# q, k and the shared expert's first products, from plain F32 to three F32R products each

## The chip, the cores and the metric

The kernel runs on one core of a Trainium2 chip, as one launch. The metric is the device time of that launch in microseconds. TensorE has two clock levels, 1.2 and 2.4 GHz; the profile gives the granted one as a share of the higher.

## The reference, cut to what matters

The model has two layers over x of shape (8, 512, 256). Only the first layer is touched:

```python
h = _layernorm(x, axis=-1) * (1 + ca) + sa
# attention of layer 0
normed = (h - mu) * rsqrt(var + LN_EPS) * ln_g + ln_b
hh = silu(normed @ W_hidden + b_hidden)      # 256 -> 1024: v and gate
qk = silu(normed @ W_qk + b_qk)              # 256 -> 512
q = qk * os_gamma[0] + os_beta[0]
k = qk * os_gamma[1] + os_beta[1]
sim = einsum('bid,biD->bdD', q, k) / seq_len
attn = softmax(sim, axis=-1)
out = v * sum(attn, axis=-1)[:, None, :] * gate
x = x + ga * (out @ W_out + b_out + h)
# experts of layer 0
h = _layernorm(x, axis=-1) * (1 + cb) + sb
shared_out = silu(h @ sw1) * (h @ sw3) @ sw2           # 256 -> 512 -> 256
# router: sigmoid(h @ router_w.T), top 2 of 8 experts, gates from their scores
# routed: gelu(h @ ew1[e]) @ ew2[e], 256 -> 256 -> 256, weighted by the gates
x = x + gb * (shared_out + routed_out)
```

The second layer is a state-space scan (512 channels, 16 states) and a gated MLP with ternary weights.

## The kernel before

Work goes by batch, 512 tokens each, eight batches in each layer. Each engine has one queue of instructions, laid when the program is built. A stage of a batch is a generator that yields a place (a due time) ahead of each piece of work; `in_order` merges all stages of an engine by these places, so the constants in `PLAN`, `PLAN_A` (first layer) and `PLAN_LAST` (its last batch's experts) fix the order and nothing else. Data is handed on by semaphores; waits stand in the code ahead of each instruction. A piece whose place is smaller than that of the one before it in the same stage follows it at once.

One batch of the first layer, on TensorE: `att_tensor` turns the normed tokens (`xhatA`, line 229), makes q/k products (four tiles of 128 tokens, line 234), the hidden products (eight tiles, lines 765 to 767), `sim` (four tiles) and the output products (`wo`). `ffn_tensor` turns `xhatF`, makes the router's products, the shared expert's first two matrices (`shared(m)`, four tiles each of `s1` and `s3`), the ranks of the routed tokens, and the shared expert's second matrix (line 1107). `experts_tensor` goes through 15 tiles of 128 routed tokens in eight pairs: step i transposes the tokens of pair i (line 1135), makes the first products of pair i-1 and the second of pair i-2. The expert steps of a batch are interleaved with the attention of the next one; those of the last batch run beside the start of the second layer.

The hidden products are already made in three F32R products. F32R (float32r) is a rounded form of float32 that TensorE takes as operand. The weights are parted once into `w_hidH` (rounded to F32R) and `w_hidL` (the rest), the input per batch into `nTH` and `nTL`, and a product is

```python
pe.matmul(bank[:, :], w_hidH[:, k, of], nTH[:, k, :], start=(k == 0), stop=False)
pe.matmul(bank[:, :], w_hidL[:, k, of], nTH[:, k, :], start=False, stop=False)
i = pe.matmul(bank[:, :], w_hidH[:, k, of], nTL[:, k, :], start=False, stop=(k == KD - 1))
```

The activation engine (ACT) makes `nT` (float32) and `nTH`; GpSimd subtracts them for `nTL` (line 681) and adds `b_out` rows to `h_tok`, multiplies and adds the k rows (`k_tok`, lines 693 and 697). DVE does the norms, the bias of q/k (line 632), the q rows (lines 636 and 640), the maxima of `sim` (line 645), the gated rows (line 656), the routing (lines 887 to 968), the product of the shared tiles (line 977) and the combination of the routed results (lines 1001 to 1006).

Routing: `slots` (line 968) releases eight indirect scatters on GpSimd (line 860) that write the normed tokens by expert into DRAM. SP loads them back as `xs` (line 815) for the expert steps; results go to DRAM as `eo_rows` (line 821), and eight indirect gathers (line 868) bring them to their tokens, for the combination. Expert weights are fetched by SP for each tile into one of `WE` = 6 buffers `w_exp`, the first matrix (line 839) when the first products of tile w - WE are done, the second (line 845) when its second products are.

PSUM banks go round in rings of four, one for attention (`att_bank`, in the order of `ATT`), one for the experts (`ffn.take`): each take waits until the reader of four tiles ago is done. `rowsA` holds a batch's shift, scale and gate rows, two buffers. `w_hid` lies in expert buffers before it is parted.

## Time and profile before

| | |
|---|---|
| Time, median of 3 runs | 2521.0 us (2517.49 to 2522.68) |
| Profiled execution, its own time | 2522.81 us |
| Its span in the trace | 2521.1 us |
| TensorE (PE) busy | 2271.8 us, 90% |
| DVE, ACT, GpSimd (POOL) busy | 1706.7, 1395.1, 1329.0 us |
| Mean granted clock of TensorE | 0.949 |

The first layer takes about the first third of the span: the last batch's tokens for attention are turned at 726.9 us, and the second layer's scans begin at 873.3 us. Times in rows are from the span's start. PE is a matmul, PEld its weight load, which lies beside it. The end of a matmul is modelled, so the pace is read from start to start.

### The profile page before, as it was taken

To read this page: it belongs to the slowest core of one execution; us is meant where nothing else is said; L and a number is where in the kernel's file an instruction comes from. 1 tells how busy PE (TensorE), PEld (TensorE's weight loads), DVE (VectorE), ACT (ScalarE), POOL (GpSimd) and SP (SyncE) were. 2 spreads that over 40 slices of the span, in tenths; PEclk is the share of its full clock that TensorE was granted. 3 is DMA by queue.
4 is the path that set the end of the run, shared out by engine and by line. 5 is a ranking of instruction groups with operands and counts; after the bars stand their busy time and mean duration, and the time that the engine had idled before them with its cause. 6 is when DMAs were issued, how large, how long until landed. Compare 5 with 4: busy or idle time off the path is not lost. (4 is left out here: it accounts for less than half of the span.)

```text
span 2521.1 us, 27219 instructions
## 1 busy us (share of the span) xinstructions
PE 2271.8 (90%) x8584; PEld 1477.0 (59%) x8584; DVE 1706.7 (68%) x2735; ACT 1395.1 (55%) x1872; POOL 1329.0 (53%) x1152
## 2 busy tenths in 40 slices
PE   7899999999999867689979989989989998988978
PEld 3576776766766532245645645655655654655666
DVE  6465655545654488996896796797787788687630
ACT  3244343443443555467677677767767667766622
POOL 4225234243251254666666665765755756767733
PEclk9899999999999987889989999999999999999989
DMA  7165465554544644545645645744744645546622
GB/s 255 64 191 174 142 200 164 179 169 135 171 143 149 217 140 132 134 125 162 170 114 162 167 127 152 186 124 137 194 116 137 185 120 155 173 125 175 167 77 92
DMA packets 253775, 384.53 MB, mean 153 GB/s; under 512 B 19168, under 2 KB 160112, under 8 KB 253632
## 3 DMA queue, kind: packets, MB, share of 16 engines
q1 hardware_dynamic: 223408, 281.07, 39.0%
q0 software_dynamic: 30224, 101.73, 13.0%
q8 instruction: 69, 1.13, 0.2%
q14 instruction: 74, 0.61, 0.1%
HBM read 345.67 MB, written 47.55 MB: 156 GB/s over the span
## 5 line engine op out<-in xcount | busy, mean ns | idle before, releaser
L1508 POOL TENSOR_TENSOR d_in<-u,bc 128x512 f32<-128x512 f32 x512 | 656.4, 1292 | 356.0 <-DMA bc<-bc_rows 294.6
L1518 DVE TENSOR_TENSOR_SCAN bank<-bank,d_in 128x512 f32<-128x512 f32 x512 | 625.9, 1222 | 114.4 <-ACT bank L1574 85.2
L1596 PE MATMUL bank<-w_st,ident 128*128 128x512 f32 x1024 | 541.3, 643 | 88.0 <-DVE w_st L1526 87.6
L1574 ACT ACTIVATE bank<-dt,a_neg 128x512 f32<-128x512 f32 x512 | 347.4, 688 | 398.3 <-DVE w_st L1526 396.7
L1526 DVE TENSOR_TENSOR w_st<-bank,bc 128x512 f32<-128x512 f32 x512 | 345.1, 674 | 136.4 <-PE bank L1596 136.0
L240 PE MATMUL bank<-f1H,w_ring 128*128 128x512 f32 x768 | 355.2, 463 | 37.0 <-POOL f1L L1674 16.1
L1596 PEld LDWEIGHTS bank<-w_st,ident 128*128 128x128 f32 x1024 | 196.6, 201 | 306.8 <-DVE w_st L1526 173.6
L241 PE MATMUL bank<-f1L,w_ring 128*128 128x512 f32 x768 | 307.7, 401 | 0.0
L240 PE MATMUL bank<-f0H,w_ring 128*128 128x512 f32 x512 | 230.8, 451 | 4.1 <-POOL f0L L1674 3.6
L1674 POOL TENSOR_TENSOR f0L<-mid,f0H 128x512 fp32r<-128x512 f32 x128 | 168.9, 1320 | 111.5 <-DVE f0H L1702 79.0
L240 PEld LDWEIGHTS bank<-f1H,w_ring 128*128 128x128 f32 x768 | 148.8, 194 | 110.7 <-issue 59.5
L241 PE MATMUL bank<-f0L,w_ring 128*128 128x512 f32 x512 | 206.7, 404 | 0.0
L204 POOL TENSOR_TENSOR norm_rstd<-norm_veps,minus_half 128x4 f32<-128x4 f32 x24 | 24.5, 1020 | 335.6 <-DVE norm_veps L200 335.6
L241 PEld LDWEIGHTS bank<-f1L,w_ring 128*128 128x128 f32 x768 | 148.9, 194 | 53.4 <-issue 25.9
L1574 ACT ACT_TABLE_LOAD x123 | 157.8, 1283 | 2.2
L240 PEld LDWEIGHTS bank<-f0H,w_ring 128*128 128x128 f32 x512 | 101.2, 198 | 43.9 <-issue 18.2
L234 PE MATMUL bank<-f_both,w_s 128*128 128x512 f32 x256 | 125.8, 649 | 0.0
L234 PE MATMUL bank<-hT,w_in 128*128 128x512 f32 x256 | 120.8, 602 | 3.9 <-ACT hT L1389 3.9
L234 PE MATMUL bank<-e_buf,w_exp 128*128 128x128 f32 x960 | 119.2, 277 | 4.2 <-DMA w_exp<-L_ffn_ew 3.2
L991 DVE TENSOR_SCALAR e_buf<-bank,mod_T 128x256 f32<-128x256 f32 (+1 forms) x128 | 61.3, 520 | 87.7 <-PE bank L1135 87.7
L234 PE MATMUL bank<-w_exp,e_buf 128*128 128x256 f32 x480 | 114.3, 382 | 7.0 <-ACT e_buf L1047 7.0
L241 PEld LDWEIGHTS bank<-f0L,w_ring 128*128 128x128 f32 x512 | 100.6, 197 | 34.1 <-issue 13.7
(222 smaller groups left out, 3898.8 us busy)
## 6 DMA issues: line engine op xcount, KB each, us to landing
bc<-bc_rows SPq DMA_DIRECT2D x256, 512.0 KB, 5.1
w_ring<-w_units POOLq DMA_DIRECT2D x160, 512.0 KB, 4.2
w_exp<-L_ffn_ew SPq DMA_DIRECT2D x240, 256.0 KB, 4.5
eo_rows<-eo SPq DMA_DIRECT2D x56, 256.0 KB, 4.9
xs<-xs_rows SPq DMA_DIRECT2D x24, 512.0 KB, 5.9
w_units<-h_T SPq DMA_DIRECT2D x16, 512.0 KB, 5.5
xA<-L_attn_x SPq DMA_DIRECT2D x8, 512.0 KB, 3.9
x_mid<-xA SPq DMA_DIRECT2D x8, 512.0 KB, 2.8
```

Of the source, the lines that this page charges most:

```text
L204: pool.tensor_tensor(norm.rstd[:, :], norm.veps[:, :], minus_half[:, :], ALU.pow).then_inc(norm.rstd_made.sem, 1)
L234: i = pe.matmul(out_, lhs(k), rhs(k), start=(k == 0), stop=(k == nk - 1))
L240: pe.matmul(out_, weights(k), hi(k), start=(k == 0), stop=False)
L241: i = pe.matmul(out_, weights(k), lo(k), start=False, stop=(k == nk - 1))
L991: j = dve.tensor_scalar(xsT[:, i % 2, o:o + n], experts_ring(b).bank["xs", b, i][:, o:o + n], mod_col(0, b, CB, k), mod_col(0, b, SB_, k), ...
L1508: pool.tensor_tensor(d_in[:, nth(b, s) % IN, :], u[:, c, :], rows_tile(b, use)[:, 0, :], ALU.mult).then_inc(in_made.sem, 1)
L1518: dve.tensor_tensor_scan(bank[:, :], bank[:, :], d_in[:, nth(b, s) % IN, :], 0.0, ALU.mult, ALU.add).then_inc(scanned.sem, 1)
L1526: dve.tensor_tensor(w_st[:, nth(b, s) % WG, :], state_bank(b, s)[:, :], rows_tile(b, step(s)[2])[:, 1, :], ALU.mult).then_inc(weighed.sem, 1)
L1574: act.activation(state_bank(b, s)[:, :], dt[:, c, :], ACT.Exp, scale=a_neg[:, c, n:n + 1]).then_inc(dA_made.sem, 1)
L1596: pe.matmul(y_bank(c)[:, :], ident[:, :], w_st[:, nth(b, s) % WG, :], start=False, stop=(n == NST - 1)).then_inc(summed.sem, 1)
L1674: pool.tensor_tensor(lo, f_full[:, i % 2, :], hi.bitcast(F32), ALU.subtract).then_inc(low_made.sem, 1)
```

## The change

- The q/k products and the shared expert's first two matrices are made of three F32R products each. `w_qk`, `w_s1` and `w_s3` are loaded into expert buffers and parted once (`parts_scalar`, `parts_pool`) into high and low parts; ACT makes `fTH` beside `fT`, GpSimd makes `fTL` by subtraction. For q/k all high products of the four tiles come first, then all low ones; the shared expert's first pair of tiles likewise.
- Buffers: `nT` lies in the place of the q rows, `fT` in two tiles of `s_act`, the SiLU is written to `s_act` in place of `s_tmp`, `WE` is 5 in place of 6, the shift and scale rows have one buffer and a load of their own, the gate rows two.
- ACT makes `nTH` ahead of `nT` for each half.
- Most places of `PLAN_A` and `PLAN_LAST` are new, and `rows_in` of `PLAN`.

```diff
-    gate_pe_first=92, rows_pe=100, dt_pe_first=98, dt_pe_second=-5.4, gate_pe_second=17, rows_in=3.2, input=2.5,
+    gate_pe_first=92, rows_pe=100, dt_pe_first=98, dt_pe_second=-5.4, gate_pe_second=17, rows_in=4.8, input=2.5,
...
-    units_in=56.2, rstd1=49, rstd2=39, rows_first=-46, rows_l0=-1, parts_high=3, parts_low=1.5, rows_l1=13.4,
-    rows_turn=23.0, n_low=-0.1, unit=7.0, stretch=1.87, after=72.0, last=55.2, last_gap=2.4, turn=68.2, x_in=53.1,
-    rows_in=62, rates=37.1, stats1=50, norm1=46.9, stats2=43.8, norm2=41.8, q_mul=7.1, q_add=9.2, sim=13.5,
-    sim_max=15.4, sim_exp=15.0, gated=16.7, wo=24.9, wo_add=26.2, f_stats=29.9, f_rstd=36.7, f_norm=34.7, f_turn=38,
-    fT=39.4, router=39.4, r_sig=52.7, route=36.0, shared=37.1, s1_act=25.7, s_mul=40.4, rank=43.2, slots=43.9,
-    s2=51.2, s2_out=51.8, scatter=48.5, xs_in=2.9, w_list=5, w_first=7.5, w_second=-1.2, xsT=0.3, e_act=1.2,
-    eo_out=9.9, gather=3, combine=8.7, x_out=14, experts=(6, 10, 12.2, 17, 20, 22.4, 25.5, 28, 33.5, 36))
+    units_in=56.2, rstd1=49, rstd2=41.9, rows_first=-46, rows_l0=-2.2, parts_high=(-12, 3, 20, 21), parts_low=(-12,
+    1.5, 20, 21), f_low=19.8, s_low=42, qk_low=2.2, rows_l1=13.4, rows_turn=23.0, n_low=-0.1, unit=7.0,
+    stretch=1.87, after=72.0, last=55.2, last_gap=2.4, turn=68.2, x_in=53.6, rows_in=62.3, rates=9.3, stats1=50,
+    norm1=46.9, stats2=43.8, norm2=41.8, q_mul=5.5, q_add=9.2, sim=14.6, sim_max=16.8, sim_exp=17.0, gated=23,
+    wo=24.9, wo_add=26.2, f_stats=36.2, f_rstd=36.7, f_norm=33.2, f_turn=38, fT=36.2, router=39.6, r_sig=52.7,
+    route=36.0, shared=37.1, s1_act=27.5, s_mul=38.6, rank=43.2, slots=38.9, s2=51.2, s2_out=50.6, scatter=48.9,
+    xs_in=2.9, w_list=5, w_first=7.5, w_second=-3.5, xsT=1.5, e_act=0.2, eo_out=7.9, gather=3, combine=8.6,
+    x_out=14, experts=(6, 10, 12.2, 17, 20, 22.4, 25.5, 28, 33.5, 36))
...
-            WE, EO = 6, 3
+            WE, EO = 5, 3
...
-            rowsA = [sb(f"rowsA{i}", [P, 3, D]) for i in range(2)]
+            rowsA = sb("rowsA", [P, 2, D])
+            gaA = [sb(f"gaA{i}", [P, 1, D]) for i in range(2)]
...
+            nT = qk_tok[:, 0, 0:KD, :]
...
+            fT = s_act[:, KS - KD:KS, :]
...
             def parts_pool():
-                yield x1_at(0) + PLAN_A["parts_low"]
-                pool.wait_ge(w_hid_split.sem, 1)
-                pool.tensor_tensor(w_hidL[:, :, :], w_hid, w_hidH[:, :, :].bitcast(F32), ALU.subtract).then_inc(w_hid_split.sem, 1)
+                for n, (whole, high, low) in enumerate(parted):
+                    yield x1_at(0) + PLAN_A["parts_low"][n]
+                    pool.wait_ge(w_high.sem, n + 1)
+                    pool.tensor_tensor(low[:, :, :], whole, high[:, :, :].bitcast(F32), ALU.subtract).then_inc(w_low.sem, 1)
...
+                sp.wait_ge(*h_step.all(b - 1))
+                sp.dma_start(rowsA[:, :, :], mod_rows[0, b, SA:CA + 1].partition_broadcast(P)).then_inc(shift_in.sem, 16)
...
+                    if t == 0:
+                        dve.wait_ge(*n_low.all(b))
                     dve.tensor_tensor(q_tok[:, t, :], k_tok[:, t, :], os_rows[:, 0, 0, :], ALU.mult).then_inc(q_step.sem, 1)
...
                 for t in range(TT):
                     yield x1 + 2 + t
-                    products(tile(2 + t)[:, :], lambda k: nT[:, k, t * P:(t + 1) * P], lambda k: w_qk[:, k, :], KD
-                             ).then_inc(qk_done.sem, 1)
+                    bank, of = tile(2 + t), slice(t * P, (t + 1) * P)
+                    for k in range(KD):
+                        pe.wait_ge(*nT_made.at(b, 2 * k + 1))
+                        pe.matmul(bank[:, :], nTH[:, k, of], w_qkH[:, k, :], start=(k == 0), stop=False)
+                        pe.matmul(bank[:, :], nTH[:, k, of], w_qkL[:, k, :], start=False, stop=False)
+                for t in range(TT):
+                    yield x1 + PLAN_A["qk_low"] + 0.5 * t
+                    for k in range(KD):
+                        if t == 0:
+                            pe.wait_ge(*n_low.at(b, k + 1))
+                        i = pe.matmul(att_bank(b, 2 + t)[:, :], nTL[:, k, t * P:(t + 1) * P], w_qkH[:, k, :], start=False,
+                                      stop=(k == KD - 1))
+                    i.then_inc(qk_done.sem, 1)
...
+                for k in range(KD):
+                    yield x1_at(b) + plan_of(b)["f_low"] + k
+                    pool.wait_ge(*fT_made.at(b, KD + k + 1))
+                    pool.tensor_tensor(fTL[:, k, :], fT[:, k, :], fTH[:, k, :].bitcast(F32), ALU.subtract).then_inc(f_low.sem, 1)
                 for j in range(TOP * TT):
...
-                    act.activation(s_tmp[:, m % 2, :], ffn.bank["s1", b, m][:, :], ACT.Silu).then_inc(s1_act.sem, 1)
+                    act.activation(s_act[:, m, :], ffn.bank["s1", b, m][:, :], ACT.Silu).then_inc(s1_act.sem, 1)
...
+                    with_high(s1, w_s1H, w_s1L)
+                    if m == 0:
+                        with_high(s3, w_s3H, w_s3L)
+                        yield x1 + plan_of(b)["s_low"]
+                    with_low(s1, w_s1H).then_inc(s1_done.sem, 1)
+                    if m:
+                        with_high(s3, w_s3H, w_s3L)
+                    with_low(s3, w_s3H).then_inc(s3_done.sem, 1)
```

`with_high` makes, for both halves k, the products of the high and of the low weights with `fTH`; `with_low` those of the high weights with `fTL`, after `f_low`.

## Rows read from the trace of the kernel before

**Rows 1.** Stretches: us, busy PE, PEld, DVE, ACT, POOL; granted clock, DMA share, GB/s.
```profile
100.00:700.00 600.00, 576.92 (x2687) 417.68 (x2686) 328.31 (x813) 242.09 (x353) 215.72 (x174) 0.98 0.53 167
294.00:304.00 10.00, 10.00 (x31) 5.07 (x31) 4.50 (x29) 2.98 (x5) 6.82 (x8) 0.83 0.28 79
800.00:900.00 100.00, 85.82 (x376) 57.17 (x376) 52.66 (x110) 58.67 (x82) 30.64 (x27) 0.98 0.59 187
```
**Rows 2.** TensorE's waits from 60 to 720 us: total, times, longest.
```profile
PE bank L1107 <- DVE s_act L977: 5.6, 5, 1.1
PE bank L234 <- DVE vg_T L656: 3.4, 1, 3.4
```
**Rows 3.** Timeline of TensorE in a middle batch: start, us, instruction, idle before.
```profile
290.86 1.09 PE L229 MATMUL bank<-ident,xhatF 128*128 128x128 f32 x8 [0.34 <-DVE xhatF L209]
...
305.21 7.11 PE L234 MATMUL bank<-f_both,w_s 128*128 128x512 f32 x16
312.16 2.75 PE L1107 MATMUL bank<-w_s,s_act 128*128 128x256 f32 x12
...
320.46 1.04 PE L229 MATMUL bank<-ident,xhatA 128*128 128x128 f32 x8
322.65 7.13 PE L234 MATMUL bank<-w_qk,nT 128*128 128x512 f32 x16 [1.15 <-ACT nT L707]
...
331.02 0.60 PE L1135 MATMUL bank<-ident,xs 128*128 128x128 f32 x4
...
332.16 0.40 PE L765 MATMUL bank<-nTH,w_hidH 128*128 128x512 f32 x1
...
336.82 0.39 PE L767 MATMUL bank<-nTL,w_hidH 128*128 128x512 f32 x1
...
365.12 0.60 PE L1135 MATMUL bank<-ident,xs 128*128 128x128 f32 x4
...
369.07 0.60 PE L1135 MATMUL bank<-ident,xs 128*128 128x128 f32 x4
```
**Rows 4.** Timeline of ACT, the same batch.
```profile
321.15 1.44 ACT L707 ACTIVATE nT<-bank,lnc 128x512 f32<-128x512 f32 x2
```
**Rows 5.** Timeline of GpSimd, the same batch.
```profile
295.05 1.05 POOL L868 DMA_INDIRECT xs<-eo_rows,slots  x1 [5.77 <-DMA eo_rows<-eo]
...
303.94 0.95 POOL L868 DMA_INDIRECT xs<-eo_rows,slots  x1 [0.31 <-issue]
308.33 1.00 POOL L860 DMA_INDIRECT xs_rows<-xhatF,slots  x1 [3.44 <-DVE slots L968]
...
323.35 2.50 POOL L681 TENSOR_TENSOR nTL<-nT,nTH 128x512 fp32r<-128x512 f32 x2 [4.54 <-ACT nTH L710]
```
**Rows 6.** Timeline of DVE, behind the last `sim` tile.
```profile
367.96 0.68 DVE L645 TENSOR_REDUCE smax<-bank 128x1 f32<-128x512 f32 x1
...
370.09 2.74 DVE L656 SCALAR_TENSOR_TENSOR vg_T<-vg_T,attn_sum 128x512 f32<-128x512 f32 x4
```
**Rows 7.** Timeline of SP's queue.
```profile
322.77 0.36 SPq L815 DMA_DIRECT2D xs<-xs_rows  x1
```
**Rows 8.** Landing of the two `xs` loads, 300 to 335 us.
```profile
DMA to landing us min/median/max: 4.1/5.1/6.0
```
**Rows 9.** Landing of a `w_exp` load at 358.4 us, the first of its burst.
```profile
DMA to landing us min/median/max: 2.9/2.9/2.9
```
**Rows 10.** Timeline of TensorE, last batch's experts.
```profile
873.50 1.13 PE L234 MATMUL bank<-e_buf,w_exp 128*128 128x128 f32 x8 [2.68 <-DMA w_exp<-L_ffn_ew]
```
**Rows 11.** Landing of a `w_exp` load at 865.8 us.
```profile
DMA to landing us min/median/max: 7.6/7.6/7.6
```
**Rows 12.** Timelines of GpSimd and of TensorE, first batch.
```profile
28.04 4.51 POOL L469 TENSOR_TENSOR w_hidL<-w_exp,w_hidH 128x2048 fp32r<-128x2048 f32 x1
...
48.60 11.65 PE L234 MATMUL bank<-qk_tok 128*128 128x512 f32 x21 [4.54 <-issue]
```
**Rows 13.** The q rows' products on DVE, line 636: duration ns min/median/max.
```profile
L636 DVE TENSOR_TENSOR qk_tok<-qk_tok,os_row_t x32: 680/686/2898, 32.4 to 741.9; 128x512 f32<-128x512 f32 x32
```

More of the change, by code:

```diff
@@ L706, in att_scalar @@
                         act.wait_ge(qk_weights_in.sem, 6 * 16)
[L707 to L711 removed]
+                    for part in (nTH, nT):
+                        act.activation(part[:, k, :], bank[:, :], ACT.Identity, bias=lnc[:, 1, k:k + 1], scale=lnc[:, 0, k:k + 1]
+                                       ).then_inc(nT_made.sem, 1)
                 for t in range(TT):
@@ L1015, in ffn_scalar @@
                         act.wait_ge(*mod_stored.all(0))
+                    if b and k == 0:
+                        act.wait_ge(*s2_done.all(b - 1))
                     act.activation(fT[:, k, :], ffn.bank["fT", b, k][:, :], ACT.Identity, bias=mod_col(0, b, SB_, k),
+                                   scale=mod_col(0, b, CB, k)).then_inc(fT_made.sem, 1)
+                for k in range(KD):
+                    act.activation(fTH[:, k, :], ffn.bank["fT", b, k][:, :], ACT.Identity, bias=mod_col(0, b, SB_, k),
                                    scale=mod_col(0, b, CB, k)).then_inc(fT_made.sem, 1)
```

140 lines of the change are left out of this document (71 added, 69 removed).

## The prediction

> **What bounds the kernel.** I read the stretches first. From 100 to 700 us, all of it in the first layer, TensorE is busy 577 of 600 us, with DVE at 328 and GpSimd at 216 [rows 1]. The change touches the first layer's products, so TensorE's waits there come next: 5.6 us in five times for the last shared product on DVE, and 3.4, once, for the gated rows [rows 2]. So in the first layer TensorE sets the pace, work taken from it comes back one for one, and a new wait on it is lost one for one. One stretch differs: between 800 and 900 us TensorE is busy only 86, because the last batch's experts and the second layer's first scans follow each other by waits [rows 1].
>
> **The products.** A plain F32 product runs as two records. Eight of the shared expert's take from 305.21 to 312.16, that is 6.95 us [rows 3]. The F32R products already in the kernel come every (336.82 − 332.16) / 20 = 0.233 us [rows 3]; 24 of them, three for each of the eight, are 5.59 us. One set of eight gives back 1.36 us. A batch has three such sets (q/k, and two of the shared expert), eight batches 24. The first batch's q/k set gives nothing (below). 23 x 1.36 = **−31.3 us**.
>
> **Orders worked out from the due times.** All queues are laid by the sorted places, so I sorted the new ones. What moves in a middle batch: on DVE the slot computation goes ahead of the second shared product, and the combination of the previous batch goes behind the fourth; on TensorE the fourth `sim` tile goes between the expert steps 4 and 5, where before both `sim` tiles came ahead of step 4; on GpSimd the two new subtractions of `fTL` go ahead of the eight gathers of the previous batch.
>
> 1. The combination stood before the fourth shared product and held it; that wait goes: **−5.6 us** [rows 2]. Nothing waits instead: the scalar copy of the shared result needs the combination, about 6 us of DVE work, while TensorE still has the 7 us of the second matrix.
> 2. q/k start. TensorE turned the tokens at 320.46 and waited 1.15 us for the two `nT` [rows 3]. Now it starts on the first half of `nTH` after one activation (0.72) [rows 4], has 0.47 us of products, and then waits for the third activation. Worked through, q/k ends as late as before, less the 1.36, plus 0.16. `nTL` comes from two GpSimd subtractions, 2.50 together [rows 5], ready some 5 us after the turn, when the high products still run to 6.2. Seven times 0.16: **+1 us**; bounds 0 and 1.2 each.
> 3. The second shared product on DVE now stands behind the slot chain, which ended 2.9 us after the rank matmuls (305.21, and the first scatter that it releases at 308.33, less 0.2) [rows 3, 5], and its bank is wanted by the fourth tile after 2.8 us of products. With the product's own 0.7 that is a wait of about 0.6: **+4 us** in seven batches. The lower bound is nothing.
> 4. The gated rows. From the last `sim` tile DVE and ACT need from 367.96 to 370.09 + 2.74, that is 4.9 us, until the four gated rows stand [rows 6]. Before, two expert steps of 3.95 (365.12 to 369.07) [rows 3] lay over it; now there is one. 4.9 − 3.95 = 1.0, seven times: **+7 us**; bounds 0 and 1.5 each, the upper with another operation of DVE in front.
> 5. The routed rows. Slots → eight scatters → load of `xs` → first expert transposes. The scatters began at 308.33, `xs` was issued at 322.77 [rows 5, 7] and the first of the two loads landed in 4.1 us [rows 8], at 326.9; the transposes came at 331.02 [rows 3]: 4.1 us to spare. This batch fell into a stretch at a lower clock (0.83 over 294 to 304 us) [rows 1], which cost TensorE about 1.7 us ahead of the slots. Without it the eight gathers, which start at 295.05 and go every 1.27 (to 303.94) [rows 5], end at 305. The two subtractions hold them until about 296.4 (turn at 290.86 [rows 3], four activations of 0.72, then 2.5), so they end at 306.5 and the scatters start no earlier than before, while TensorE reaches the transposes 4.4 us earlier: a set ahead of the rank, a set behind it, q/k, and the wait of point 1, less points 2 and 3. 4.4 − 4.1, with something for scatters that stretch: 0.5, six times: **+3 us**; bounds 0, and 2.4 each when the load takes the 6.0 of the second one.
> 6. Five expert buffers instead of six. The second tile of a pair now waits for the down products of two pairs ago instead of three. In a middle batch a `sim` or output tile (3.45) lies between, with transposes and the first tile's products 4.8 us in all; a load at the head of its burst lands in 2.9 after 0.3 on the queue [rows 9]. **0**; it turns at 4.5 us of landing.
> 7. The last batch. Its expert steps follow each other, and at 873.50 TensorE has already waited 2.68 us for weights [rows 10]. Between the release and the need lie 1.3 us, so with 0.3 + 2.9 each of five steps waits 1.8 more; with the backlog that gave 7.6 us [rows 11] it is over 4, but longer steps also thin the backlog, and some of the wait was there before. I take **+6 us**; bounds 0 and +13. The second layer's sums stand behind these steps in TensorE's queue, so this comes through.
> 8. The first batch. GpSimd parts `w_hid` in 4.51 us, and the q and k rows follow there; TensorE is idle 4.54 us before `sim` at 48.60 for them [rows 12]. The split of `w_qk`, half as large, is added in front, about 2.3 on GpSimd, in part in its earlier idle time: **+1 us**, and the q/k saving of this batch is lost there. The later splits of `w_s1` and `w_s3` lie where GpSimd has nothing to do.
> 9. Hand-over. The second layer's first norm sits among the last batch's gathers on GpSimd, which don't move with the last two shared sets (2 x 1.36 = 2.7): I take somewhat less than half of that as lost, **+1 us**; bounds 0 and 2.7.
> 10. The rest at nothing: the `rowsA` load parted in two is one issue more on SP, 0.5 us, a dozen microseconds ahead of use; two more activations a batch (1.5) lie on an ACT busy 242 of 600 us [rows 1]; the second layer's `rows_in` moves one row store ahead of one load.
>
> The sum is −31.3 − 5.6 + 1 + 4 + 7 + 3 + 0 + 6 + 1 + 1 = −13.9. The profiled execution took 2522.8 (span 2521.1), 1.8 above the median 2521.0. 2521 − 14 = **2507 us**.
>
> **Ports.** `q_mul` on DVE takes 680 ns at best and 2898 at worst, on tiles of one form, and GpSimd's two passes on `k_tok` run beside it [rows 13]. The Trainium skill, "SBUF — State Buffer", section "SBUF: two separate sides", says that a DVE operation with two SBUF inputs and a GpSimd operation that reads SBUF hold one port pair in turn, each for its whole length. By that rule the new subtractions can hold DVE for up to 2.5 us in a batch; the trace agrees that such pairs stretch each other. If the routing chain met both in all eight batches, the time would be 20 us more, 2527; I give that 0.03, inside the slower side's chance, and leave it out of the sum, because the subtractions end about when the sigmoid comes.
>
> **Rivals.**
> - *The saving arrives nearly whole.* The new waits of points 3, 4, 5 and 7 are all derived from margins of 1 to 2 us; if they don't open, −31.3 − 5.6 + 3 = −34: 2487, and with half of them 2497. For it: the 577 of 600. Against it: point 4 is plain addition. 0.17.
> - *Routing swallows it.* The chain of point 5 doesn't get shorter, since GpSimd's gathers and scatters set it. If `xs` lands in 6 us and the scatters go by 1.35 instead of 1.27, the wait is about 2.9, six times 17 instead of 3: 2521, no change. For it: GpSimd works through gathers and scatters without a gap in such a batch. 0.19.
> - *Slower: five buffers starve the experts.* If the loads at the head of a burst land in 6 instead of 2.9 (7.6 was seen with the scans' loads beside them [rows 11]), each of four steps in seven batches waits 1.5, 42 in all with the tail's +13 in place of +6: 2556 at the worst. It decides from about 5.2 us of landing, where 28 waits of 0.7 eat the gain. Against it: the 2.9, with 1.9 to spare. With the port case, 0.16.
> - The forecast, 2498 to 2516: 0.48.
>
> That the products don't get faster is excluded by the 0.233 of the same form beside them.
>
> **How the numbers follow.** 0.2% is 5 us, about what a measurement of this kernel can tell from no change. Faster (below 2516): 0.48 + 0.17 = 0.65. Same: 0.19. Slower: 0.16. The range leaves out the worst of both ends: 2491 to 2525.
>
> **What would show it.** Three records per product at 0.233 on the q/k and shared lines, and no 128x512 F32 product on them; 31 us less TensorE work in the first layer. New waits: output products for `vg_T` about 1 us a batch, the fourth shared tile for `s_act`, transposes of `xs` at most 1; in the last batch `w_exp` waits of 10 us or so together. The second layer from first scan to end should last as long as before. I'm wrong if first-layer transposes wait 2 us or more in each batch, if `w_exp` waits appear in the middle batches, or if the second layer's own length moves.

## The result, and the profile after

The kernel after takes **2545.1 us** (median of 4, 2540.9 to 2549.7), the kernel before 2520.8 (median of 4): ratio **1.0098** [1.0074, 1.0122], slower by 24 us. Forecast were 2507 and a range of 2491 to 2525. One thing has to be said ahead, since no number below can be read without it: in other sessions the very same file took 2519.3 to 2519.7, three times. What the sessions differ in is the theme of half the experiments. A completion is TensorE's signal that its product is done, for which DVE or ACT waits. I call a session *clean* where the trace has a record of each of the sixteen landings of every gather (128 in a batch), and all 1414 completions of TensorE stand within 0.1 us of where their matmuls end. In a *late* session 31 to 58 of the 128 landing records are there in each of the first seven batches, and 26 to 38 of the 1414 completions come later than that, by 0.2 to 10 us, or have no record. The recorded result is from a late session.

The page's first lines of the kernel after:

```profile
span 2540.1 us, 27696 instructions
...
PE 2251.9 (89%) x8776; PEld 1519.4 (60%) x8776; DVE 1708.6 (67%) x2735; ACT 1427.2 (56%) x1906; POOL 1358.0 (53%) x1171
```

TensorE does its work in 20 us less than before (2251.9 against 2271.8), and the span is 19 us longer: what was saved came back as idle time, and more. The stretches of [rows 1] show the place, the first of the two being the first layer:

```profile
100.00:700.00 600.00, 557.23 (x2791) 443.26 (x2790) 327.62 (x811) 261.22 (x370) 226.08 (x181) 0.97 0.53 166
800.00:900.00 100.00, 81.66 (x399) 61.13 (x397) 43.63 (x112) 47.12 (x69) 26.21 (x25) 0.97 0.56 182
```

In the first of them TensorE is idle 43 of 600 us where it was idle 23. Its waits from 60 to 720 us (in total, times, longest) answer to [rows 2]:

```profile
PE bank L1113 <- DVE s_act L1005: 11.0, 5, 2.8
PE bank L235 <- DVE vg_T L677: 9.5, 7, 3.4
...
PE bank L774 <- ACT nTH L729: 8.7, 12, 1.7
...
PE bank L235 <- DVE e_buf L1019: 3.0, 1, 3.0
PE bank L1113 <- issue: 3.0, 1, 3.0
PE bank L1157 <- DVE s_act L1005: 2.1, 1, 2.1
PE bank L1157 <- issue: 0.9, 1, 0.9
```

And the same view of the same file in a clean session (e4, below):

```profile
PE bank L235 <- DVE vg_T L677: 9.5, 7, 3.4
...
PE bank L1113 <- DVE s_act L1005: 3.2, 7, 0.5
PE bank L1157 <- DVE s_act L1005: 3.1, 1, 3.1
PE bank L235 <- DVE e_buf L1019: 3.0, 1, 3.0
```

The second list is the one to hold against the forecast: for `vg_T` 6.1 more than before, in six new waits of 1.0 (point 4), and 3.2 at the fourth shared tile (point 3), both as worked out. The two single waits of 3 us, at L1157 for `s_act` and at L235 for `e_buf`, are not in the forecast. What the first list has above the second, at L1113 and L1157, is the late session's.

**Where the time lies.** I cut the first layer at TensorE's two kinds of turns: A, the tokens' (`ident,xhatA`, start of a batch), and F, the second norm's (`ident,xhatF`, start of its shared expert). The "65th scan" is the start of DVE's 65th 128x512 scan of the second layer. All numbers are differences of starts, in us. "Before, clean" is e0 and "after, clean" is e4, two clean sessions.

| stretch | before, clean | after, clean | after, recorded |
|---|---|---|---|
| to the first F | 88.1 | 92.3 | 91.0 |
| seven A to F, sum | 500.8 | 504.1 | 505.8 |
| seven F to A, sum | 211.3 | 191.4 | 215.3 |
| last F to 65th scan | 244.5 | 255.3 | 253.6 |
| 65th scan to end | 1475.8 | 1474.5 | 1474.4 |
| span | 2520.6 | 2517.6 | 2540.1 |

So there are two questions. Why does the kernel in a clean session gain 3 us of span and not 14? By stretch the change is +4.2, +3.3, −19.9, +10.8 and −1.3. And why does the recorded run stand 22.5 us above the clean one? Nearly all of it, 23.9, lies between F and A.

### The profile page after: what moved, and what is told of

The parts are those of the page before. It is cut to its first block and busy times, and to the rows that moved or that the text cites. A ratio compares the mean times of both kernels' runs of the same rounds, so it can differ in the third digit from the quotient of the medians.

```text
span 2540.1 us, 27696 instructions
## 1 busy us (share of the span) xinstructions
PE 2251.9 (89%) x8776; PEld 1519.4 (60%) x8776; DVE 1708.6 (67%) x2735; ACT 1427.2 (56%) x1906; POOL 1358.0 (53%) x1171
## 5 line engine op out<-in xcount | busy, mean ns | idle before, releaser
L235 PE MATMUL bank<-e_buf,w_exp 128*128 128x128 f32 x960 | 120.7, 278 | 10.9 <-DMA w_exp<-L_ffn_ew 7.9
L235 PE MATMUL bank<-hT,w_in 128*128 128x512 f32 x256 | 122.1, 607 | 3.9 <-ACT hT L1439 3.9
L235 PEld LDWEIGHTS bank<-e_buf,w_exp 128*128 128x128 f32 x960 | 114.8, 194 | 12.9 <-DMA w_exp<-L_ffn_ew 6.4
L1076 ACT ACTIVATE e_buf<-bank 128x512 f32<-128x512 f32 x64 | 36.4, 571 | 152.1 <-PE bank L235 152.0
L235 PE MATMUL bank<-qk_tok 128*128 128x512 f32 x256 | 115.2, 600 | 3.9 <-issue 3.9
```

The lines of the kernel that those rows point to most:

```text
L235: i = pe.matmul(out_, lhs(k), rhs(k), start=(k == 0), stop=(k == nk - 1))
L1076: act.activation(e_act[:, i % 2, 0:n], experts_ring(b).bank["up", b, i][:, 0:n], ACT.Gelu).then_inc(e_act_made.sem, 1)
```

## The experiments

### The same kernels again, and the signals

The first session repeated the kernel before (e0) and ran the kernel after with its three new signals defined behind all others (e1) and with two signals fewer (e2), in case the places of the semaphores had to do with the missing records. It was a clean session.

```
-            shift_in = signal("shift_in", 16)
-            w_high, w_low = signal("w_high"), signal("w_low")
+            w_high = signal("w_high")
-            f_low = signal("f_low", KD)
+            shift_in = signal("shift_in", 16)
...
+            w_low, f_low = signal("w_low"), signal("f_low", KD)
```

That was e1. This is e2, in which the waits on the joined signals are raised to the common count:

```
-        a_log_in, a_step = signal("a_log_in"), signal("a_step", 2)
-        mlp_scales_in, units_in = signal("mlp_scales_in"), signal("units_in")
+        a_log_in = mlp_scales_in = ssm_weights_in
+        a_step, units_in = signal("a_step", 2), signal("units_in")
```

> The kernel before, profiled once more beside the others. In the changed kernel's profile the rank matmuls' end reaches VectorE about 2 us later than TensorE's record of it, in six batches, and only a part of the 16 landings of each gather and scatter is on record. If that belongs to the chip or to the profiling, it must show here too; if it belongs to the changed program, here VectorE starts the slots within 0.1 us of the rank's end and the time stays at 2521.

> The changed kernel with its new signals made last, so that those of the gathers, scatters and shared products are the ones that they are in the kernel before; as many signals in use as in the changed kernel. Theory A (the late completions come with the particular signals that the change moved): the delay of about 2 us behind the rank goes, the time falls by 20 or more, to about 2520. Theory B (they come from something else in the changed program, such as the places of the tiles, the products or the order): no change, 2545 within 5.

> The changed kernel with three signals of early loads made one, so that it uses two signals fewer and as many as the kernel before. Theory A' (the two more signals in use are the cause, whichever they are): the delay behind the rank goes, about 2520. Theory B: no change, 2545 within 5.

Measured: e0 2522.3; e1 2519.1, ratio 0.9989 [0.9977, 1.0002]; e2 2522.8, 0.9999 [0.9988, 1.0009]. Both lack the 24 us. That looked as if the signals were the cause, until the unchanged file ran in another session:

> The changed kernel once more, unaltered. In its own profile TensorE's completions came late beside gathers and scatters and most landings of these were not on record; in the three altered forms of it that ran since, one of them with all the signals as they are in the changed kernel, none of this was seen. Theory D (it belongs to the chip or to the executions of that session, not to the program): no late completion here, and 2520 to 2523, as with the form that only uses two signals fewer. Theory A (it belongs to exactly this program): late completions and 2540 to 2550 again.

2519.5, ratio 0.9985 [0.9972, 0.9998]. Nothing in the file had changed, so the signals had nothing to do with it, and the difference is one of sessions. The unchanged file ran three times more:

> The changed kernel unaltered once more, on the same chip as e10. If the first profile's late completions are rare or belonged to one chip: none here, ratio 0.997 to 1.000. If they come back in one session of a few: F32R products or not, the stretches from the second norm's turn to the tokens' turn grow by 3 to 4 us each in the middle batches, the ratio is 1.007 to 1.012.

> The changed kernel unaltered. Late completions beside the gathers, as in the first session: 2540 to 2550, F32R or not, and most landings of gathers and scatters off the record. Without them: 2517 to 2521, as on three chips so far.

> The changed kernel unaltered beside e14. Undisturbed: 2517 to 2521 and every landing on record; disturbed: 2535 to 2550, and the rank's end reaches VectorE 2 us late in the middle batches.

| run | session | after | ratio | F to A, sum |
|---|---|---|---|---|
| recorded | late | 2545.1 | 1.0098 [1.0074, 1.0122] | 215.3 |
| e4 | clean | 2519.5 | 0.9985 [0.9972, 0.9998] | 191.4 |
| e11 | clean | 2519.3 | 0.9987 [0.9977, 0.9997] | 193.1 |
| e13 | late | 2539.5 | 1.0057 [1.0040, 1.0075] | 217.5 |
| e15 | clean | 2519.7 | 0.9992 [0.9978, 1.0007] | 191.4 |

e13 was on the chip of e4, at a later time, so it isn't the chip either. Within one session all traces were of one kind. The count of landing records tells the session; in the view of the DMA groups it shows as a group without its landing time, first after as recorded, then e4:

```profile
xs<-eo_rows,slots POOLq DMA_INDIRECT x64
```
```profile
xs<-eo_rows,slots POOLq DMA_INDIRECT x64, 2.8
```

### What the late session does, and why the kernel before is spared

One middle batch, after as recorded. TensorE, then DVE, ACT and GpSimd:

```profile
298.61 1.09 PE L230 MATMUL bank<-ident,xhatF 128*128 128x128 f32 x8 [0.34 <-DVE xhatF L210]
...
309.11 1.04 PE L1146 MATMUL bank<-rt,ones 128*128 128x8 f32 x8
...
315.31 0.50 PE L1113 MATMUL bank<-fTH,w_s1H 128*128 128x512 f32 x1 [2.26 <-DVE s_act L1005]
...
317.75 0.63 PE L1119 MATMUL bank<-fTL,w_s3H 128*128 128x512 f32 x2
319.29 2.83 PE L1157 MATMUL bank<-w_s,s_act 128*128 128x256 f32 x12 [0.90 <-issue]
...
324.24 6.27 PE L1157 MATMUL bank<-w_s,s_act 128*128 128x256 f32 x20 [2.13 <-DVE s_act L1005]
```
```profile
311.99 0.22 DVE L970 TENSOR_TENSOR over<-bank,tile_edge 128x64 f32<-128x64 f32 x1 [3.30 <-issue]
...
323.50 0.69 DVE L1005 TENSOR_TENSOR s_act<-bank,s_act 128x512 f32<-128x512 f32 x1 [4.31 <-remote]
```
```profile
321.26 0.60 ACT L1058 ACTIVATE s_act<-bank 128x512 f32<-128x512 f32 x1 [5.11 <-remote]
```
```profile
301.50 2.52 POOL L879 TENSOR_TENSOR fTL<-s_act,fTH 128x512 fp32r<-128x512 f32 x2 [4.47 <-ACT fTH L1049]
304.18 1.05 POOL L898 DMA_INDIRECT xs<-eo_rows,slots  x1 [0.16 <-issue]
...
313.08 0.94 POOL L898 DMA_INDIRECT xs<-eo_rows,slots  x1 [0.30 <-issue]
314.94 1.00 POOL L890 DMA_INDIRECT xs_rows<-xhatF,slots  x1 [0.91 <-DVE rt L992]
```

The same stretch in e4, TensorE and DVE:

```profile
310.41 1.04 PE L1146 MATMUL bank<-rt,ones 128*128 128x8 f32 x8
...
314.80 0.50 PE L1113 MATMUL bank<-fTH,w_s1H 128*128 128x512 f32 x1 [0.45 <-DVE s_act L1005]
...
317.70 7.07 PE L1157 MATMUL bank<-w_s,s_act 128*128 128x256 f32 x32
324.61 1.04 PE L230 MATMUL bank<-ident,xhatA 128*128 128x128 f32 x8
```
```profile
311.49 0.23 DVE L970 TENSOR_TENSOR over<-bank,tile_edge 128x64 f32<-128x64 f32 x1 [1.49 <-PE bank L1146]
```

In e4 the slot chain begins 0.04 us behind the end of the rank matmuls (310.41 + 1.04 = 311.45). As recorded it begins at 311.99, 1.84 behind 310.15, with "issue" for a releaser: DVE waits for a completion that by the matmuls is long there. The chain, the next shared product and the fourth tile all shift: TensorE waits 2.26 us for the fourth tile where it waited 0.45. The late completion of the ranks falls within GpSimd's eight gathers (304.18 to 314.02). Then the last tile's `s1` product is finished at TensorE at 317.0, and ACT starts on it only at 321.26; the `s3` product is finished at 318.38, and DVE starts on it only at 323.50. Both are released by "remote", which costs TensorE 2.13 more. These two come late among the eight scatters (from 314.94). From F to A this batch takes 31.7 us, in e4 24.7.

As recorded, six of the first seven batches start the chain 1.2 to 2.5 us late, in e13 likewise 1.15 to 2.45; in e4 and e11 all seven start within 0.04. (The other one is the first batch, which has no gathers. The eighth starts 1.0 to 1.1 behind in every run, clean or late.) The last `s1` tile is late in four batches, two in each of the two late runs, by 4.3, 4.3, 9.8 and 10.5 us. These are the four in which the first scatter follows the last gather within 1 us; in the others of the first seven it is late by 0.1 at most.

From 60 to 810 us TensorE's waits at L1113 come to 15.6 us as recorded and to 3.6 in e4, those at L1157 to 8.1 and 3.1, those for `nTH` to 11.4 and 8.4. That is 20 of the 22.5 us.

Is that this change's doing, or a plain property of such a session that its kernel before would show too? One late session has the kernel before with one constant altered, `WE, EO = 5, 3` for `6, 3` (e12, meant for point 6, below); another has that (e16) and the kernel before itself:

> The kernel before, one profile. If the session is disturbed: the rank's end reaches VectorE in time (gathers done), which is why this kernel is spared, and only part of the landings is on record. If undisturbed: all as in e0.

Measured: 2525.4, a single run with span 2523.7, 31 of 1414 completions not in their place (after as recorded: 38), and landing records missing as in e13. So the late completions come in the kernel before too. Yet its F to A sum is 211.4, that of e0 is 211.3: it pays nothing there. From the last F to the 65th scan it takes 248.0 where e0 takes 244.5, so there the late session may cost it 3.5. Its times beside e13 (2524.0, median of 15) and beside e16 and e17 (2521.0, of 7) are close to those beside clean traces (2519.8 to 2523.0). The same sections of e12 and e16, both late and both in the old order, are 213.7 and 210.1. The rows of one batch:

```profile
409.42 1.04 PE L1096 MATMUL bank<-rt,ones 128*128 128x8 f32 x8
```
```profile
412.52 0.22 DVE L940 TENSOR_TENSOR over<-bank,tile_edge 128x64 f32<-128x64 f32 x1 [2.95 <-remote]
```
```profile
409.91 0.95 POOL L868 DMA_INDIRECT xs<-eo_rows,slots  x1 [0.30 <-issue]
```

The chain begins 2.06 us late here (412.52 against 410.46), but that is the worst batch; three others have 0.76, 0.47 and 0.16. In the middle batches the last gather ends 12.6 to 14.8 us after F and the rank matmuls end 12.8 to 16.6 after F, so mostly the gathers are over when the completion is sent, and DVE has the combination and no slot chain in front of TensorE's need. In the kernel after, the faster products bring the rank's end forward (11.5 to 14.7 after F as recorded), and the two `fTL` subtractions hold the gathers until 15.4 to 15.7: the rank's end lies inside the gathers in each of these batches, and by the new order the fourth tile of TensorE hangs on it.

The three late runs of the old order bear this out batch by batch. Where the rank's end comes 1.9 us or more behind the last gather (five middle batches of e12, e16 and e17), the chain starts within 0.04. Where it comes at most 1.5 behind, or inside, the chain is late in all thirteen, by 0.2 to 2.1. So in late sessions overlap with the gathers and lateness go together; in clean ones the same overlap costs nothing (e4). What delays a completion is not shown. Nor is it separated how much of the late session's cost hangs on the overlap and how much on the new order: the new products with the old order (e3) met only a clean session.

The Trainium skill, "NOTIFIC — the notification-queue block", section "7.1 Overflow: three behaviours, one of which stalls the engine", says that a full queue of records either drops new ones, overwrites old ones or holds the producer until software has read. Missing landing records would fit the first, late completions the third, and the section lets a queue do only one of them. Every execution here was recorded, so no run here shows whether records are the cause at all.

### The parts of the change, in clean sessions

**The new order on DVE.** e3 has F32R products, but the old places of the slot chain, the products and the combination:

```
-    route=36.0, shared=37.1, s1_act=27.5, s_mul=38.6, rank=43.2, slots=38.9, s2=51.2, s2_out=50.6, scatter=48.9,
-    xs_in=2.9, w_list=5, w_first=7.5, w_second=-3.5, xsT=1.5, e_act=0.2, eo_out=7.9, gather=3, combine=8.6,
+    route=36.0, shared=37.1, s1_act=27.5, s_mul=40.4, rank=43.2, slots=43.9, s2=51.2, s2_out=50.6, scatter=48.9,
+    xs_in=2.9, w_list=5, w_first=7.5, w_second=-3.5, xsT=1.5, e_act=0.2, eo_out=7.9, gather=3, combine=8.7,
```

> The changed kernel with the old due times of three steps of VectorE: the second shared product ahead of the slots again, and the combination ahead of the fourth. Theory C (the new order costs the time: TensorE's fourth shared tile waits for a product that is behind the slots, 11 us in all, and then again for the third and fourth): the waits of the fourth tile go, 11 us less, and about as much again if the waits of the last shared matrix are their consequence, so 2525 to 2535. Theory B: the fourth tile also waits for the slots themselves, which start late anyway, so the time stays within 5 of 2545, and the old wait for the last product, 5.6 us, comes back: 2545 to 2550.

2532.6, ratio 1.0045 [1.0026, 1.0065], some 13 us above the kernel after. The wait that point 1 took away is back, and larger (5.6 in five before):

```profile
PE bank L1157 <- DVE s_act L1005: 16.3, 5, 4.1
```

**The shared expert's products alone.** e5 leaves q and k as F32R and makes the shared products plain F32 again, without `fTL`:

```
-                    with_high(s1, w_s1H, w_s1L)
...
+                    products(s1[:, :], lambda k: w_s1H[:, k, of], lambda k: fTH[:, k, :], KD)
```

> The changed kernel with the shared expert's two first matrices multiplied in plain F32 again (16 products of two records each, no low part of the inputs, no two subtractions ahead of the gathers); q and k, the buffers and the due times stay as changed. The shared sets then cost 2 x 1.36 us a batch more, 22 in all. Theory P (the products bring what they save): 22 slower than the changed kernel, less the wait of the fourth tile and what the earlier gathers give back, so about 15 slower than e4. Theory R (routing behind the gathers sets the pace of this section, so that the saving there is swallowed): within 5 of e4.

2538.3, ratio 1.0061 [1.0042, 1.0080]: 18.8 us over e4, beside 16 × 1.36 = 21.8 by the forecast's price of a set, less what the plain form is spared. The products do give what the sum says. In e4 one set from its first record (306.80) to the next instruction (309.60) takes 2.80 for twelve products, 0.233 each.

**Four sites that the forecast missed or priced too low.** Each was undone alone, in one clean session, whose kernel-before median is 2522.0. In e6 the combination of batch 1 goes behind the fourth product, in e7 the decay rates of the second layer go away from batch 1's start, in e8 two copies of the last batch go ahead of the `dt` chain, in e9 the first batch has q and k as plain F32. Only the changed parts of the lines stand here:

```
-    gather=3, combine=8.6,
+    gather=3, combine=8.65,
```
```
-    rates=9.3, stats1=50,
+    rates=37.1, stats1=50,
```
```
-    rank=39.1, e_act=2.2, eo=1.6, eo_out=8.7, gather=19.7,
+    rank=39.1, e_act=1.7, eo=1.6, eo_out=8.2, gather=19.7,
```
```
                 if b == 0:
-                    pe.wait_ge(w_low.sem, QK_PARTS)
-                for t in range(TT):
+                    pe.wait_ge(*nT_made.all(0))
+                    for t in range(TT):
+                        yield x1 + 2 + t
+                        products(tile(2 + t)[:, :], lambda k: nT[:, k, t * P:(t + 1) * P], lambda k: w_qk[:, k, :], KD
+                                 ).then_inc(qk_done.sem, 1)
+                for t in range(TT if b else 0):
```

> The changed kernel with the combination due 0.05 later. In seven of eight batches nothing moves; in batch 1 the two due times are equal to rounding, the combination stands ahead of the fourth shared product there, and TensorE waits 3.1 us for it at 221 us in e4, then runs at the low clock. Theory (this order is the cost): the wait goes, from the turn of the second norm to the next turn of tokens batch 1 takes 25 to 27 us, as the other batches, instead of 31, and the whole 3 to 5 us less than e4. Rival (the combination only waits for late gathers and the fourth product is then held by the slots): within 1 us of e4 in that stretch.

> The changed kernel with the second layer's rates prepared at the old place in batch 1 again (due 37.1 instead of 9.3). In e4 these five operations, 4.1 us on VectorE, stand ahead of the second expert input of batch 1, TensorE waits 3.0 us for it, and from turn to turn of norms batch 1 takes 75.8 us against 71.4 in the others. Theory (they are the cost): 71.4 to 72 there, 4 us less in all, less what they cost at the old place beside the slots (0 to 2). Rival (the fifth expert step of batch 1, 4.5 us later than in the others, comes from its weights or rows): still 75.

> The changed kernel with the old due times of the last batch's expert copies (e_act and eo_out 0.5 earlier). In e4 ScalarE does the step size's chain of the second layer, 6 us, ahead of the copy of an expert result, and TensorE waits 5.6 us for that at 882 us. Theory (the order is the cost): that wait goes; the step size comes later by 0.6 and TensorE then waits for the next activation as before (1.9), so 3 to 4 us less than e4. Rival (the second layer's first steps wait for the step size, not for the experts): the sums start as late as in e4, 22.4 us behind the first scan, no change in the whole.

> The changed kernel with q and k of the first batch alone in plain F32 products on the undivided weights. In e4 TensorE waits 3.2 us for the low part of the weights of q and k, and the first batch ends 4.2 us later than in the kernel before, where 1 was forecast. Theory (the division ahead of them is the cost): q and k start 2.2 us earlier, and the second norm's turn comes 2 to 4 us earlier, at 88.5 to 90 us. Rival (GpSimd is the bound of the first batch, with the two divisions, the inputs' low part and the rows of k, 2.5 us more than before): still 91.5 to 92.5.

| run | time | ratio | section | there |
|---|---|---|---|---|
| e6 | 2521.0 | 0.9985 [0.9972, 0.9999] | batch 1, F to A | 26.3, was 28.0 to 31.0 |
| e7 | 2517.3 | 0.9980 [0.9967, 0.9994] | batch 1, A to F | 71.3, was 75.8 to 77.5 |
| e8 | 2516.4 | 0.9986 [0.9968, 1.0003] | last F to 65th scan | 252.9, was 254.2 to 255.6 |
| e9 | 2520.7 | 0.9993 [0.9976, 1.0010] | to the first F | 87.4, was 87.7 to 92.6 |

No one of them can be told from e4 by its time. By the sections e6 and e7 do what they were meant to, though in e7 the five moved operations now stand in batch 1's F to A, which takes 31.5. In e8 TensorE's wait for `eo` is gone, but the section is only 1.3 to 2.7 shorter, and in e14 below, with the same two due times, it is 255.0: what that order costs isn't shown. e9 doesn't leave the scatter of the others. The rows of e4 behind them: batch 1's start on TensorE and DVE,

```profile
145.92 3.35 PE L235 MATMUL bank<-e_buf,w_exp 128*128 128x128 f32 x16 [3.00 <-DVE e_buf L1019]
```
```profile
140.77 1.28 DVE L580 TENSOR_SCALAR a_neg<-a_neg 128x64 f32<-128x64 f32 x1
141.97 2.95 DVE L583 TENSOR_SCALAR skip_diag<-ident,d_skip 128x128 f32<-128x128 f32 x4
144.84 0.98 DVE L1019 TENSOR_SCALAR e_buf<-bank,mod_T 128x256 f32<-128x256 f32 x2
```

where five operations of the second layer's preparation now stand ahead of an `xs` copy that TensorE wants; batch 1's shared part on DVE,

```profile
214.90 3.26 DVE L1029 SCALAR_TENSOR_TENSOR f_tok<-xs,gates,f_tok 128x256 f32<-128x256 f32 x8 [1.76 <-DMA xs<-eo_rows,slots]
218.19 1.23 DVE L1032 TENSOR_TENSOR f_tok<-f_tok,gate_row 128x1024 f32<-128x1024 f32 x1
219.45 1.22 DVE L1034 TENSOR_TENSOR xA<-xA,f_tok 128x1024 f32<-128x1024 f32 x1
220.59 0.68 DVE L1005 TENSOR_TENSOR s_act<-bank,s_act 128x512 f32<-128x512 f32 x1
```

where the two due times are equal but for rounding, so that in this one batch the combination still stands ahead of the fourth product (TensorE waits 3.08); the last batch on TensorE and ACT,

```profile
868.71 3.55 PE L235 MATMUL bank<-e_buf,w_exp 128*128 128x128 f32 x16 [3.12 <-DMA w_exp<-L_ffn_ew]
...
881.60 0.69 PE L1185 MATMUL bank<-ident,xs 128*128 128x128 f32 x2 [5.60 <-ACT eo L1085]
```
```profile
877.63 1.06 ACT L1421 ACTIVATE cv<-cv 128x1024 f32<-128x1024 f32 x1
...
880.96 0.58 ACT L1085 ACTIVATE eo<-bank 128x512 f32<-128x512 f32 x1
```

where the copy of an expert's result now stands behind the second layer's `dt` chain; and the first batch,

```profile
26.47 0.80 PE L774 MATMUL bank<-w_qkH,nTH 128*128 128x512 f32 x1 [3.16 <-POOL w_qkL L483]
```
```profile
23.93 2.48 POOL L483 TENSOR_TENSOR w_qkL<-w_exp,w_qkH 128x1024 fp32r<-128x1024 f32 x1 [3.78 <-ACT w_qkH L499]
```

**All four, and the subtractions moved.** e10 joins the four. e14 adds one thing, the two `fTL` subtractions on DVE, ahead of the routing, in place of GpSimd, which frees the gathers to start at once:

```
-                for k in range(KD):
-                    yield x1_at(b) + plan_of(b)["f_low"] + k
-                    pool.wait_ge(*fT_made.at(b, KD + k + 1))
-                    pool.tensor_tensor(fTL[:, k, :], fT[:, k, :], fTH[:, k, :].bitcast(F32), ALU.subtract).then_inc(f_low.sem, 1)
...
                 yield x1 + plan_of(b)["route"]
+                for k in range(KD):
+                    dve.wait_ge(*fT_made.at(b, KD + k + 1))
+                    dve.tensor_tensor(fTL[:, k, :], fT[:, k, :], fTH[:, k, :].bitcast(F32), ALU.subtract).then_inc(f_low.sem, 1)
```

> The changed kernel with the four corrections of e6 to e9 together. Alone, by their profiles against those of the unaltered kernel, they gave 1.7 to 4.7 us from the second norm's turn to the tokens' turn of batch 1 (e6), 4.5 to 6 in batch 1 (e7), 2.6 between the last batch's turn and the 65th scan (e8) and 3 to 5 in the first batch (e9). If they add up: 11 to 15 less than the changed kernel of the same call, 12 to 16 less than the kernel before, ratio 0.9935 to 0.9955. If they share one cover (the clock's stretches fall elsewhere and take part of it back): 5 to 8 less than the changed kernel.

> The kernel of e10 with the two subtractions that make the low part of the shared inputs on VectorE instead of GpSimd, so that the gathers start some 2.7 us earlier behind the second norm's turn, as in the kernel before. If the session is undisturbed: the routing chain on VectorE starts about 0.5 us later and TensorE's fourth tile has 0.5 to 1 more to wait in seven batches, but the combination and the scatters have slack: 2507 to 2512, within 4 of e10's 2509. If late completions are back: theory L (they strike completions that fall within the gathers' time, so that earlier gathers shield the slots' start) has this kernel lose at most half of what the changed kernel loses; rival (any completion from the second norm's turn on is struck) has it lose the same, 15 to 20.

e10: **2509.3**, ratio 0.9958 [0.9944, 0.9971], 10 us under the kernel after in the same session (e11). e14: **2507.6**, 0.9947 [0.9932, 0.9961], 12 us under e15 beside it. Both beat both kernels; between themselves their intervals overlap, so the moved subtractions show no gain of their own in a clean session. In the middle batch of e14 whose F is near 292 us the gathers run from 295.68 to 305.64 and the rank matmuls end at 305.47, so the slot chain starts with the gathers all but over. Whether that spares e14 in a late session is open, since it never met one; in e12, e16 and e17 a rank's completion within 0.5 us of the last gather's end was still 0.9 to 2.1 late.

**Five buffers alone.** The kernel before with one constant altered:

```
-            WE, EO = 6, 3
+            WE, EO = 5, 3
```

> The kernel before with five expert buffers instead of six and nothing else changed. The forecast priced this at nothing in the middle batches and at 6 us in the last one (0 to 13). Theory: from turn to turn of norms the middle batches stay at 71.6 and 27.9 to 31.3, and from the last second norm's turn to the 65th scan it takes 249 to 253 instead of 244.5 to 245.1, so the whole 4 to 8 slower. Rival (the ten us that the changed kernel loses there come from the order of the expert copies and loads, not from the fifth buffer): 245 to 247, no change in the whole.

> The kernel before with five expert buffers once more, to have its cost without the late completions that its first session (e12) had. From e12's profile, in stretches that hold no gather: 1.3 us in each of seven middle batches (TensorE waits 1.45 for w_exp there) and 10 us from the last second norm's turn to the 65th scan. If those are the buffer's own: 15 to 20 slower than before here too, ratio 1.006 to 1.008. If they came with the disturbed session: within 5 of before.

2541.1, 1.0065 [1.0050, 1.0079], and 2542.4, 1.0082 [1.0065, 1.0099]. Both ran in late sessions. A to F is 72.8 to 73.0 in the middle batches against 71.6, where e17, late like them, has 71.6 too: this is the buffer's. The last F to the 65th scan is 252.8 (e16) and 254.8 (e12); e17, in e16's session, has 248.0 and e0 244.5, so the buffer costs 4.8 to 6.8 there against a late kernel before, and the rest may be the session's. TensorE's waits in e12 from 60 to 810 us, and one of them in the timeline:

```profile
PE bank L234 <- DMA w_exp<-L_ffn_ew: 10.2, 7, 1.5
...
PE bank L1107 <- DVE s_act L977: 7.6, 6, 1.6
```
```profile
374.56 0.60 PE L1135 MATMUL bank<-ident,xs 128*128 128x128 f32 x4
...
377.45 1.16 PE L234 MATMUL bank<-e_buf,w_exp 128*128 128x128 f32 x8 [1.40 <-DMA w_exp<-L_ffn_ew]
```

In the order of the kernel before, two expert steps follow each other here, and the fifth buffer is missed in each middle batch, by some 1.45 us. In the new order a tile of attention stands between them, and no such wait is seen (A to F 71.3 to 71.4 in e4).

## Why the prediction was wrong

The recorded 2545 lies outside the range, and "faster" was the wrong side. Two separate things failed: in late sessions waits that the forecast priced at 4 us and at nothing, which alone outweigh the gain; and in clean sessions points 8, 10 and the hand-over, which leave 2 to 4 of the 14 us.

**In late sessions** the kernel takes 20 to 26 us more. In the prediction's own terms the steps that failed are point 3 and "nothing waits instead" of point 1. Point 3 took it that the slot chain starts when the rank matmuls end, and priced the fourth tile's wait at 4 us; the chain started 1.2 to 2.5 us late in six batches, and the waits at L1113 came to 15.6 (3.6 in e4). Behind it, where point 1 had no wait, those at L1157 came to 8.1 (3.1 in e4, all of it batch 1's). None of the rivals has this: "routing swallows it" named the right chain but another link (the gathers' end before the scatters). I had put "two subtractions ahead of the eight gathers" and "the slot chain ahead of the second product" side by side, each with its own price, and didn't ask what the second is exposed to by the first. The lateness itself couldn't be read from a profile of before, which was clean. Why a session is late, and what holds a completion, stays open. So does whether it exists with no record taken, and whether the clean profile of before, three of whose times are among the four that the result is compared with, was taken beside the recorded run or apart from it. Shown is that it isn't the file (five runs), nor the chip (e4 and e13), nor the signals (the unaltered file is as clean in e4 as e1 and e2 were), and that the kernel before, in which the same lateness is seen, isn't lengthened between F and A.

**In clean sessions** the time was 2519.3 to 2519.7, −2 to −4 by the three ratios where −13.9 was summed. Point by point:

- *Products, and points 1 to 5*: right in kind. F to A came to −19.9: fourteen shared sets 14 × 1.36 = −19.0, point 1 −5.6, point 3 +3.2 (4 forecast), sum −21.4. The tie in batch 1 (below) gives back about 3. The −1.5 left over fits 3.4 us less at the lower clock (1.2 GHz) in these sections, 32.4 against 35.7. A to F of batches 2 to 7 came to −0.2 each (71.6 to 71.4, five of them): −1.36, +0.16 and +1.0 of points 2 and 4 make −0.2. The gated rows wait 1.01 to 1.02, seven times. No wait for `xs` opened (point 5).
- *Point 6*: right, and its reason too. With the old order, where no tile lies between the two steps, the fifth buffer is missed (e12, e16); the tile of attention that the point counts as margin is what hides it. The buffer is free only together with the new order.
- *Points 7 and 9, the hand-over*: it came to +10.8 where 6 + 1 − 2.7 = 4.3 was summed. Point 7 itself was sized well: `w_exp` waits went from 2.7 in one to 8.5 in four, 5.8 more where 6 was taken. What the list lacked is the copy of `eo` behind the `dt` chain, a wait of 5.6. With that wait taken out the section is 249.5 (e10), 252.9 (e8) and 255.0 (e14) against 255.3, so how much of the 6.5 is its doing stays open.
- *Point 8*: mis-sized, +4.2 in e4 where +1 was taken. `w_qkL` waits for ACT's rounding as well (3.78), so it didn't use GpSimd's earlier idle time, and its full 2.48 stands in front of q and k. By e9 and the spread of this section (87.7 to 92.6; three traces of the kernel before have 86.1 to 88.1) the size is not sure.
- *Point 10, "the rest at nothing"*, failed outright. It missed the `rates` operations in front of an `xs` copy at the start of batch 1, +4.2 in e4 and +5.9 in e11. I had sorted the places of a middle batch; batch 1 has work that no other has, and the sort would have shown it.
- *Point 1 in batch 1*: the two due times tie there but for rounding, and the combination stays in front; about 3 us, and behind it a stretch of lower clock that is counted with the clock.

Together, with what is left over taken for clock: −13.9 + 6.5 (hand-over) + 3.2 (8) + 4.2 (10) + 3 (the tie) − 3.8 (points 3 and 5, priced 0.8 and 3 too high) − 1.5 (clock between F and A) − 1.3 (second layer) = −3.6, beside −3.0 of span. Undoing the four gives 2509.3, 2 from the forecast; that it comes so near is in part luck, as points 3 and 5 were priced 3.8 too high.

**The port rule**, 0.03 in the forecast. In e4 the subtractions run from 302.81 to 305.3 and DVE's first routing operation, at 304.94, takes 0.43; in e14, with nothing on GpSimd, it takes 0.19. The Trainium skill, "SBUF — State Buffer", section "SBUF: two separate sides", has the two take turns at a port pair, and the trace agrees, but at 0.2 to 0.3 us in each of six batches (0.42 to 0.48 for 0.19) and not 2.5, since the operation meets only the end of a subtraction.

## What to carry to other kernels

Where queues are sorted by due times, sort them for each batch that is unlike the others (the first, the second, the last) and not only for a middle one: all four sites that e10 undoes were in these, and for three of them the sorted places alone would have shown it. A resource that is cut (a sixth buffer) is to be priced in the order in which it will stand, and with the order taken away too, to see which of the two carries it. And a result of one per cent on one session should be taken again in another before it is explained: the same file gave 0.9985 and 1.0098, each with an interval of a quarter of a per cent.

## What the runs showed of the hardware

- A completion of TensorE can reach its reader late: for the rank matmuls 0.2 to 2.5 us after the modelled end where it falls among indirect gathers that GpSimd issues, or at most 1.5 us behind them; for the shared expert's last tile 4 to 10 us where the scatters follow the gathers within 1 us. It is seen in 3 of the 8 sessions traced with or after the result, in both kernels, always together with missing landing records (31 to 58 of 128 are there), and not at all in the other 5 (0.04 us).
- A 128x512 subtraction of two SBUF tiles into fp32r takes GpSimd 1.25 us and DVE 0.68 (2.51 and 1.36 for two). On the engine that looked free it held the next eight DMA issues; moved to the busier one it left the time the same within the noise (e10, e14).
- Stretches at the lower clock level (1.2 GHz) between F and A cost about half their length: the same work takes 25.0 us with none, 26.5 with 3.4 us of it, 28.1 with 6.8 (e4). They come and go with the waits ahead of them, so a difference of 1.5 or 3 us in one batch proves nothing.
